# Attention stage: first spatial products ahead of the preceding group's band products on TensorE

## What is computed

```
x = x + conv(layernorm_c(x)):
  k1   = per-pixel convolution of 9 taps along the channels + bias
  a    = softmax over 9 taps( W2 relu(bn(W1 [x;k1] interleaved)) + b2 )       # the taps
  v    = depthwise 3x3 convolution of x
  out1 = sum over d of a[d] * v[channel + d - 4] + k1                         # band of 9 channels
  k1s  = relu(bn(depthwise 3x3 of x))
  a2   = softmax over 81 pixels( grouped 1x1( relu(bn(grouped 1x1([k1s;x]))) ) + b2 )
  out2 = k1s + a2 * x
  result = alpha * out1 + (1 - alpha) * out2
t = tokens(x);  t = t + mixture_of_8_experts(layernorm(t), top 2)
```

## Time and profile before

| what | value |
|---|---|
| median of 3 runs | 1621.7 us |
| profiled execution, its own time | 1627.32 us |
| its span, first to last instruction | 1625.6 us |
| mean granted TensorE clock over the span | 0.885 |
| TensorE busy | 1309.9 us (81%) |
| VectorE busy | 1087.0 us (67%) |
| ScalarE busy | 772.1 us (47%) |
| GpSimd busy | 568.0 us (35%) |

### The profile page before, as it was taken

The page is one execution under the profiler, slowest core; times in us unless marked ns, Lnnn a source line. Parts: engine busy times, 40 slices in busy tenths (PEclk is TensorE's granted clock), DMA queues, the critical chain, the costliest instruction groups (busy, mean ns, idle before and its releaser), DMA issues.

```text
span 1625.6 us, 36996 instructions
## 1 busy us (share of the span) xinstructions
PE 1309.9 (81%) x9796; PEld 1078.3 (66%) x9797; DVE 1087.0 (67%) x2553; ACT 772.1 (47%) x1828; POOL 568.0 (35%) x561
## 2 busy tenths in 40 slices
PE   0196999799999999986746501999999999999692
PEld 0186999756766666666746501888888888888531
DVE  6796555357888877874566662777777777777462
ACT  0294666344445444442576771455554545555200
POOL 0162111134433444330377775233333333333200
PEclk9997999889999999995555555999999999999896
DMA  8535566778778777661144354222222222222297
GB/s 321 139 92 192 202 241 235 252 176 188 188 170 202 179 185 189 162 148 54 54 150 135 131 179 158 76 85 91 91 91 87 84 89 90 90 91 77 85 423 310
DMA packets 258517, 251.16 MB, mean 155 GB/s; under 512 B 150009, under 2 KB 234446, under 8 KB 255204
## 3 DMA queue, kind: packets, MB, share of 16 engines
q1 hardware_dynamic: 238093, 197.20, 41.1%
q0 software_dynamic: 20320, 53.45, 9.6%
q10 hardware_dynamic: 66, 0.05, 0.0%
HBM read 152.34 MB, written 105.75 MB: 159 GB/s over the span
## 4 chain that ended last, share of the span: by engine, by line
PE 59%; DVE 15%; DMA 9%; issue 5%; ACT 5%; SPq 2%; POOL 2%; DVEq 0%; ACTq 0%; POOLq 0%
PE ps L690 15%; PE ps L675 14%; PE ps L490 5%; PE ps L470 4%; DMA u_d<-in_zstrings 3%; PE ps L659 2%; DMA pool_<-y_d 2%; PE ps L542 2%; POOL rows_d L1521 2%; PE ps L515 2%; SPq L288 2%; PE ps L525 2%; DMA pool_<-in_ffn_w 2%; ACT aux L1388 2%; PE ps L459 2%
## 5 line engine op out<-in xcount | busy, mean ns | idle before, releaser
L1530 POOL DMA_INDIRECT y_d<-pool_,to_s x176 | 173.5, 986 | 361.2 <-ACT pool_ L1447 331.9
L690 PE MATMUL ps<-pool_,aux 128*128 x2112 | 248.4, 274 | 6.2 <-DVE aux L1197 3.2
L675 PE MATMUL ps<-aux,pool_ 128*128 128x256 f16 x2112 | 246.5, 274 | 0.7 <-ACT aux L1440 0.6
L690 PEld LDWEIGHTS ps<-pool_,aux 128*128 128x128 f16 x2112 | 199.7, 98 | 49.9 <-issue 25.6
L675 PEld LDWEIGHTS ps<-aux,pool_ 128*128 x2112 | 206.2, 98 | 25.9 <-issue 1.7
L1521 POOL DMA_INDIRECT rows_d<-aux,idx_s x162 | 159.2, 983 | 105.4 <-ACT aux L1390 60.0
L1440 ACT ACTIVATE aux<-ps,b_s 128x256 f32<-128x256 f32 x352 | 138.3, 475 | 93.0 <-DVE aux L1197 92.6
L1432 ACT ACTIVATE aux<-ps 128x512 f16<-128x512 f32 x88 | 52.6, 597 | 188.8 <-PE ps L659 188.8
L1515 POOL DMA_DIRECT2D pool_<-v_d x64 | 50.0, 781 | 223.5 <-PE ps L575 220.3
L1205 DVE SCALAR_TENSOR_TENSOR pool_<-ps,pool_ 128x512 f32<-128x512 f32 x88 | 60.9, 692 | 96.0 <-PE ps L690 96.0
L515 PE MATMUL ps<-pool_,se_w_s 81*81 81x512 f32 x256 | 118.8, 608 | 6.1 <-DMA pool_<-k_d 6.1
(11 more groups left out here) (204 smaller groups left out, 3030.6 us busy)
## 6 DMA issues: line engine op xcount, KB each, us to landing
pool_<-rows_d SPq DMA_DIRECT2D x88, 260.0 KB, 2.8
pool_<-y_d SPq DMA_DIRECT2D x18, 1152.0 KB, 13.9
big<-in_x SPq DMA_DIRECT2D x2, 5184.0 KB, 21.3
xn_d<-big SPq DMA_DIRECT2D x16, 648.0 KB, 3.0
v_d<-aux SPq DMA_DIRECT2D x64, 162.0 KB, 2.1
ks_d<-aux SPq DMA_DIRECT2D x64, 162.0 KB, 2.2
pool_<-xn_d SPq DMA_DIRECT2D x32, 324.0 KB
pool_<-k_d SPq DMA_DIRECT2D x32, 324.0 KB
```

Of the source, the lines that this page charges most:

```text
L675: last = nc.tensor.matmul(o, w_s[:, a, bass.ds(e * (4 * PIECE) + (k * HID + j * 128), 128)], xh_s[:, par, b, k * SLOTS:(k + 1) * SLOTS], s ...
L690: last = nc.tensor.matmul(ps[:, 6 + par, s * C:(s + 1) * C], hh_s[:, par, a, j, s * 128:(s + 1) * 128], w_s[:, b, bass.ds(e * (4 * PIECE) ...
L1530: nc.gpsimd.indirect_dma_start(out=y_d[:, :], out_offset=bass.IndirectOffsetOnAxis(ap=to_s[:, par, k:k + 1], axis=0), in_=yo_s[:, par, k, ...
```

## The change

In `pe_turn`, the order of TensorE's steps in one turn, `spatial_1` moves ahead of `band`, in both halves of the turn. Nothing else is changed: waits, buffers and the other engines' code stay.

```
                 if front:
                     keys(2 * i, 0, i, first)
+                if front:
+                    spatial_1(2 * i, 0, i)
                 if late:
                     band(2 * i - 3, 1, i - 1)
                 if front:
-                    spatial_1(2 * i, 0, i)
                     tap_logits(2 * i, 0)
                     spatial_2(2 * i)
                 if back:
                     unmasked(2 * i - 2, 0, i)
                 if front:
                     keys(2 * i + 1, 1, i)
+                if front:
+                    spatial_1(2 * i + 1, 1, i)
                 if back:
                     band(2 * i - 2, 0, i)
                 if front:
-                    spatial_1(2 * i + 1, 1, i)
                     tap_logits(2 * i + 1, 1)
                     spatial_2(2 * i + 1)
                 if back:
```

## The result

The changed kernel takes 1655.7 us in the median of 4 runs (1649.75 to 1658.2), the kernel before 1623.0 in the same comparison (1620.54 to 1625.0): ratio 1.020, 95% interval 1.0175 to 1.0218. It is 33 us slower. Forecast was 1620.4 with a range from 1611 to 1632; the sign that was thought least likely came, by a mechanism that no rival named.

What follows compares the result with a forecast made beforehand. TensorE was taken as nearly the bound, waiting about a microsecond per turn for VectorE's mask. 2.8 us won, less 2.0 and 0.5, plus 1 for the clock: 1.3 us less, 1620.4 us, range 1611 to 1632.

Steps and rivals of the forecast that it cites:

- the sign that was thought least likely: Whole kernel: a slower result, given 0.27 in all, against 0.40 for within 0.2% and 0.33 for faster.
- The order of the waits: Attention stage: waits for exponentials and kc/xc loads now stand ahead of the band's 2.52 us, no longer behind it.
- New wait of the first half: TensorE's spatial products, first half: wait of 0.46 us for the last exponential, start at 476.48.
- End of the first half: TensorE's L534: 0.46 us later, at 482.99 in place of 482.53.
- End of the second: Second half: TensorE waits 0.63 us until 489.1, and the turn ends at 495.61 against 495.81.
- The turn: Regular turn of the attention stage: 25.07 us instead of 25.27, 0.20 won in each of 14 turns.
- VectorE's relief: VectorE's L928 and L932 run without GpSimd beside them and become short, making VectorE 1.83 us earlier per turn.
- The loads: Second half: kc and xc land 5.3 us after L932, plus 0.05 for the semaphore, and end the last wait at 489.1.
- Rival B: Second half: GpSimd's L1511 delays VectorE's L906, due 0.27 us earlier; turn 0.8 to 1.0 longer, 1633 to 1636 us; chance 0.12.
- one term of the sum: TensorE's clock: idle time in shorter pieces, one less at times of two turns lengthened by a lower clock, 1 us won.
- the two turns in which GpSimd was late by itself: Attention stage: these turns already won about 1.2 us each and have nothing left to win, counted as -2.0 us.

Runs made afterwards that it cites:

- e7: Kernel before with GpSimd's two elementwise instructions on one column in place of 648, leaving out the residual term: 1606.2 us, ratio 0.985.
- e9: Kernel before, all work kept, with GpSimd's L1508 also waiting for VectorE's L932 of the group before: 1608.6 us, ratio 0.989.
- e2: Kernel before with only the corner products moved behind the spatial products, next to the tap logits: 1650.0 us, ratio 1.016.
- e1: Changed kernel with only half 0 of the spatial products ahead of the band, half 1 behind it: 1646.4 us, ratio 1.013.
- e8: Kernel before with only the first half of the turn changed, and spatial_2 ahead of the tap logits there: 1613.9 us, ratio 0.989.
- e6: Changed kernel with GpSimd's two elementwise instructions on one column in place of 648, leaving out the residual term: 1653.8 us, ratio 1.013.
- e3: Kernel before with only the first half of the turn changed: 1621.5 us, ratio 0.997.
- e5: Changed kernel with spatial_2 ahead of the tap logits in both halves, VectorE waiting for the logits before its maxima: 1653.8 us, ratio 1.013.
- e4: Kernel before with only the second half of the turn changed: 1668.5 us, ratio 1.027.

## Why the prediction was wrong, step by step

**The order of the waits was right.** This can be read at full clock in one turn only, the one at 482.84. Times from the start of the turn's first L534. New wait of the first half: L525 forecast at 5.94, measured 5.85 (482.84 to 488.69). End of the first half: forecast 12.45, measured 12.46. End of the second: forecast 12.62 behind that, measured 12.64. The turn: forecast 25.07, measured 25.10.

**VectorE's relief was right.** L934 takes 0.89. It would have been worth 1.3 us a turn in the old order (e7, e9); in the changed order it went into the loads and exponentials, as forecast.

**The loads.** Forecast: TensorE waits for kc and xc until 5.35 us after L932. Measured: L934 ends at 496.02, L525 starts at 501.34, 5.32. The wait is there 12 times and makes 5.4 us. The 5.3 us had been picked between bounds of 5.05 and 7.36, so that it fits to 0.03 is in part luck.

**Rival B's distance held at full clock.** L908 starts at 497.94, 0.18 us ahead of L1513 at 498.12. The page "SBUF — State Buffer" of the Trainium skill, section "Who interferes with whom", calls the ports that VectorE and GpSimd share an exclusive lock; that the lock holds for the whole instruction it says beside VectorE's two-port modes, and of an instruction with two SBUF inputs only that it contends. As the prediction took it, the rule would have let L1510, drawn from 496.02 to 497.94, hold off L907; L907 started at 497.74 and took 0.17, and in the first half, at 484.88 within L1510's 483.50 to 485.41, it took 0.17 too. GpSimd's spans are rough, but in neither place does the trace follow the rule.

**What failed is one term of the sum.** The prediction wrote of the lower clock: "idle TensorE time is split into shorter pieces, and of the two turns that a lower clock lengthened I expect one less at times, worth 1 us." It tied the clock to idle time only, and asked nothing about which instructions the new order puts side by side. The runs show the opposite sign: 13 of 14 turns lengthened instead of 2, and a loss of (51 - 7) / 2 = 22 us where the term had 1 us won. e2 shows that it is not idle time: TensorE is drawn as busy without a gap there and the clock falls. What the change made neighbours is 0.7 us of corner products, 32 rows by 32 or by 4 columns, and 1.8 us of nine-column tap logits. That their standing together matters is shown by e1 and e8 (dense products between them, one fall and none) and by e2 (put together, 19 falls); why it matters no run shows.

The sum has a small slip besides: the two turns in which GpSimd was late by itself cost 2.4 us against the 2.8, not 2.0, for their 2 x 0.20 stood in the 2.8 already. Too little to matter.

**The rest of the loss, 4 to 5 us,** is waits. TensorE's drawn waits in the 14 turns are 13.6 us against 12.6, but there are 26 of them in place of 12, and a wait costs 0.26 us more than is drawn (12.64 - 11.99 - 0.40 = 0.25, 13.28 - 11.99 - 1.03 = 0.26). By this estimate the waits cost 1.0 + 14 x 0.26 = 4.6 us more than before. They are longer than forecast in the first half: behind a fall TensorE and VectorE are 1.7 and 1.1 us late, GpSimd is not, and L907 runs into L1513; the wait of the first half is then 0.65 in place of 0.20. The price of rival B came in, but in this kernel as a consequence of the clock. What it would cost with the falls held equal no run shows: in e6 it is gone, but there the falls come in nearly every half, and in e1 it is there at full clock.

**What stays open.** Why the same neighbours are followed by a fall in some turns and not in others: e2 runs seven halves without one in the same order, and e3 most of its turns. The traces show that the moment matters. In e2 the falls come 13.65 us apart (the trace has them at 634.86, 648.51, 662.16) while the slow halves take 13.71, so the first corner product, 2.8 us ahead of the fall at 413, is 2.4 us ahead of that at 495, and then the seven halves without a fall follow; what sets the moment of a fall is not shown. The two falls of the kernel before come with other neighbours, 2.2 and 2.4 us behind the end of a wait of 1.04 us for the mask. A kernel with the corner products made as dense as the others was not tried.

## What to carry to other kernels

Before moving steps in TensorE's queue, list the small products (few rows or few columns) and look which of them become neighbours: in an otherwise dense queue they can lower the clock although no engine waits, and the first place to look is the clock column of short windows. A few dense products between them were enough (e8), and cost nothing on TensorE, since the order of the two steps was free; VectorE had to wait for the later of them, and the turn stayed at 24.40 us. Longer waits of TensorE are followed by falls as well (1.76 us in e5, 2.6 in e4). And when an engine is late by a microsecond, look for two long instances of an otherwise short instruction before reordering the one that waits: here one wait on GpSimd (e9) removed the wait for the mask, which was the aim of the whole reordering, and won 17 us.

## What the hardware showed that I had not expected

- A fall of the clock mostly lasts about 3.4 us in these traces and then costs 1.67 us. In long stretches of e2 and e6 the falls come once per half turn, in the kernel after once per turn, and the halves take 13.7 us almost to the hundredth (13.68, 13.71): the loop and the falls run in step, so that a small cause can repeat turn after turn.
- GpSimd's two-input instruction (128x648) holds off a VectorE addition of 128x8 with both inputs in SBUF by 1.0 us (0.17 becomes 1.17), and one of 128x144 by 1.1 (0.31 becomes 1.41), while VectorE's instructions that read PSUM (L898, L915 and L917 of the kernel after) take 0.5, 0.4 and 0.5 us beside it as without it.
- The two costs trade places: taking the falls away (e1, half of them in e5) moved the collision, taking the collision away (e6) brought more falls, and with the kernel after all four are within 1646 to 1656 us.
